# Block-sparse attention stage: softmax denominators exchanged by a VectorE stream shuffle instead of a TensorE product, and four kinds of filler work gathered into later groups

## What is computed

```python
def make_block_sparse_mask(seq_len):
    bi = jnp.arange(seq_len) // BLOCK_SIZE            # blocks of 128
    is_global = bi % GLOBAL_EVERY == 0                # block 0
    allowed = (bi[:, None] == bi[None, :]) | is_global[:, None] | is_global[None, :]
...
scores = jnp.einsum('bhqd,bhkd->bhqk', q * scale, k) + mask
attn = jax.nn.softmax(scores, axis=-1)
out = jnp.einsum('bhqk,bhkd->bhqd', attn, v)
out = out.transpose(0, 2, 1, 3).reshape(B, L, D)
return out @ w_out.T + b_out
```

## Time and profile before

| | |
|---|---|
| median of 3 runs | 3188.89 us (3188.46 to 3190.44) |
| the profiled execution | 3189.74 us, span 3187.9 us |
| TensorE busy in the span | 3000.4 us (94%) |
| VectorE, ScalarE, GpSimd busy | 2341.2, 1703.3, 1696.9 us |
| mean granted TensorE clock | 0.978 of 2.4 GHz |

### The profile page before, as it was taken

The page is one execution under the profiler, slowest core; times in us unless marked ns, Lnnn a source line. Parts: engine busy times, 40 slices in busy tenths (PEclk is TensorE's granted clock), DMA queues, the critical chain, the costliest instruction groups (busy, mean ns, idle before and its releaser), DMA issues. The chain is left out here.

```text
span 3187.9 us, 46188 instructions
## 1 busy us (share of the span) xinstructions
PE 3000.4 (94%) x14226; PEld 1726.6 (54%) x14226; DVE 2341.2 (73%) x4175; ACT 1703.3 (53%) x3501; POOL 1696.9 (53%) x1102
## 2 busy tenths in 40 slices
PE   6999999999999988899999799999999999999997
PEld 3454545454545444455555466666666666666665
DVE  8999999999999988577775655556665555565553
ACT  4767686858586753344444344444444444444442
POOL 2666666666666655233332455555555555565552
PEclk9999999999999999899999799999999999999998
DMA  4767676767667666311010000000001200000000
GB/s 149 256 213 259 215 252 216 243 220 247 231 236 241 214 231 198 97 41 39 26 33 28 20 21 7 13 20 20 20 20 40 73 14 26 20 26 26 26 13 21
DMA packets 131300, 343.37 MB, mean 108 GB/s; under 512 B 14898, under 2 KB 57990, under 8 KB 131222
## 3 DMA queue, kind: packets, MB, share of 16 engines
q1 hardware_dynamic: 128918, 334.02, 30.9%
q10 hardware_dynamic: 2304, 8.39, 0.7%
HBM read 320.87 MB, written 21.50 MB: 107 GB/s over the span
## 5 line engine op out<-in xcount | busy, mean ns | idle before, releaser
L559 POOL TENSOR_TENSOR hb<-bcB,du 128x1024 f32<-128x1024 f32 x256 | 602.5, 2354 | 389.1 <-DVE hb L699 349.9
L688 DVE TENSOR_TENSOR_SCAN ps_dA<-ps_dA,hb 128x1024 f32<-128x1024 f32 x256 | 585.7, 2288 | 43.1 <-ACT ps_dA L914 43.1
L1226 PE MATMUL ps_y<-hb,ident 128*128 128x512 f32 x1024 | 490.4, 608 | 29.6 <-DVE hb L699 29.6
L2375 POOL TENSOR_TENSOR c_pr<-c_pr,c_inv 128x512 f32<-128x512 f32 (+1 forms) x256 | 237.3, 935 | 321.4 <-DVE c_inv L2496 321.4
L914 ACT ACTIVATE ps_dA<-delta,a_neg 128x511 f32<-128x511 f32 x512 | 330.0, 676 | 1.1
L1226 PEld LDWEIGHTS ps_y<-hb,ident 128*128 128x128 f32 x1024 | 189.5, 192 | 251.7 <-issue 186.8
L699 DVE TENSOR_TENSOR hb<-ps_dA,bcC 128x1024 f32<-128x1024 f32 x256 | 311.9, 1218 | 5.9
L2634 ACT ACTIVATE c_pr<-c_ps_s,c_negmax 128x256 f32<-128x256 f32 (+1 forms) x512 | 223.9, 452 | 147.1 <-DVE c_negmax L2489 123.7
L1785 ACT ACTIVATE b_pt<-b_ps_t 128x512 f32<-128x512 f32 x320 | 173.9, 595 | 214.6 <-PE b_ps_t L1905 214.1
L2489 DVE CUSTOM_DVE_ANT_0 c_ps_s<-c_ps_s,c_mask 128x256 f32<-128x256 f32 (+1 forms) x512 | 188.5, 418 | 120.0 <-issue 120.0
L1622 DVE TENSOR_REDUCE b_negmax<-b_ps_s 128x4 f32<-128x1024 f32 (+1 forms) x160 | 194.8, 1222 | 96.6 <-PE b_ps_s L1889 96.5
(11 more groups left out here) (314 smaller groups left out, 5904.2 us busy)
## 6 DMA issues: line engine op xcount, KB each, us to landing
bcB<-bc_scratch SPq DMA_DIRECT2D x256, 512.0 KB, 4.5
bcC<-bc_scratch SPq DMA_DIRECT2D x256, 512.0 KB, 4.6
c_x<-stream_scratch SPq DMA_DIRECT2D x16, 512.0 KB, 4.9
c_xr<-stream_scratch SPq DMA_DIRECT2D x16, 512.0 KB, 3.6
rows<-in_x_dram SPq DMA_DIRECT2D x8, 512.0 KB, 5.4
sum<-in_x_dram SPq DMA_DIRECT2D x8, 512.0 KB, 7.6
x_scratch<-sum SPq DMA_DIRECT2D x8, 512.0 KB, 6.7
b_xb<-x_scratch SPq DMA_DIRECT2D x8, 512.0 KB, 4.6
```

The costliest lines, as they stand in the source:

```text
L559: pool.tensor_tensor(hb[:, s % RING, :, :], bcB[:, s % ROWS, :, :], bc(du[:, c % 2, :].unsqueeze(1), [P, NG, T]), ALU.mult)\
L688: dve.tensor_tensor_scan(flat(h_all), flat(h_all), flat(tile), 0.0, ALU.mult, ALU.add)\
L1226: last = pe.matmul(ps_y[:, :], W["ident"][:, :], hb[:, r % RING, i, :], start=False, stop=(g == GROUPS - 1 and i == NG - 1))
L2375: pool.tensor_tensor(rows, rows, bc(inv[:, u, :].unsqueeze(2), [P, 2, w]), ALU.mult)\
```

## The change

TensorE's permutation (`swap_inverse`, the `b_swap` constant and its masks) is gone. `den` is now written first; VectorE waits for it, writes `num`, and moves `den` by 16 partitions within each 32 with a `stream_shuffle` to `inv`, where the reciprocals are taken in place. The multiplication `divide` moves to GpSimd, behind a `mask`. The product of quarter 0 with v stands in group 4, in front of quarter 1's. The transposes of the next item move to groups 3 and 4, both q/k projections of a half to group 5, all of the projection to v to group 4, its copy to group 4 and the statistics to group 5. In `last`, VectorE shuffles before it inverts and GpSimd multiplies.

```diff
-            return () if m or k > 2 else ((0,), (1, 2), (3,))[k]
-            return (0,) if k == (1 if m else 3) else (1,) if k == (3 if m else 5) else ()
+                    if more and m == 0 and k in (3, 4):
+                        uses += [("x", 2 * (k - 3)), ("x", 2 * (k - 3) + 1)]
+                    if more and k == 5:
+                        uses += [("qk", m, 0), ("qk", m, 1)]
...
+        SWAPPED = [(i + HD) % 32 for i in range(32)]
...
+            def divide(b, m):
+                pool.wait_ge(inv_ready.s, inv_ready.at(b, m + 1))
+                pool.wait_ge(out_done.s, out_done.at(b, 0))
+                pool.tensor_tensor(oT[:, m, :], num[:, :], inv[:, :], ALU.mult).then_inc(oT_ready.s, 1)
...
-                dve.scalar_tensor_tensor(num[:, :], ps_o[:, :], row_mask[:, 1:2], o_num[:, :], ALU.mult, ALU.add)
                 dve.scalar_tensor_tensor(den[:, :], ps_o[:, :], row_mask[:, 0:1], o_den[:, :], ALU.mult, ALU.add)\
                     .then_inc(out_parts.s, 1)
+                dve.wait_ge(out_parts.s, out_parts.at(b, 2 * m + 1))
+                dve.scalar_tensor_tensor(num[:, :], ps_o[:, :], row_mask[:, 1:2], o_num[:, :], ALU.mult, ALU.add)\
+                    .then_inc(out_parts.s, 1)
+                dve.stream_shuffle(inv[:, :], den[:, :], SWAPPED).then_inc(den_swapped.s, 1)
...
-                last = dve.reciprocal(inv[:, cols], den[:, cols])
+                last = dve.reciprocal(inv[:, cols], inv[:, cols])
...
-            def divide(b, m):
-                dve.wait_ge(inv_swapped.s, inv_swapped.at(b, m + 1))
-                dve.wait_ge(out_done.s, out_done.at(b, 0))
-                dve.tensor_tensor(oT[:, m, :], num[:, :], ps_s[:, 0, :], ALU.mult).then_inc(oT_ready.s, 1)
...
-                    if more and k == 5:
+                    if more and k == 4:
                         take_v(n)
-                    if more2 and k == 6:
+                    if more2 and k == 5:
                         statistics(n + 1)
...
-            def swap_inverse(b, m):
-                pe.wait_ge(inv_ready.s, inv_ready.at(b, m + 1))
-                pe.matmul(ps_s[:, 0, :], swap[:, :, :, :].rearrange("p g f d -> p (g f d)"), inv[:, :], start=True, stop=True)\
-                    .then_inc(inv_swapped.s, 1)
...
-                    if k in (2, 4, 6, 8):
+                    if k == 4:
+                        weigh(b, 0, 0, uses, b)
+                    if k in (4, 6, 8):
                         weigh(b, 0, (k - 2) // 2, uses, b)
```

More of the change, by code:

```diff
@@ L1482, in _ @@
             pool.memset(sixteenths[:, :], 0.0).then_inc(s_const, 1)
-            pool.memset(swap[:, :, :, :], 0.0).then_inc(s_const, 1)
-            pool.wait_ge(s_const, 2)
+            pool.wait_ge(s_const, 1)
             pool.affine_select(out=sixteenths[:, :], in_=sixteenths[:, :], compare_op=ALU.not_equal, fill=1.0,
                                base=0, pattern=[[-HD, 8]], channel_multiplier=1).then_inc(s_const, 1)
[L1487 to L1490, removed]
             pool.memset(negmax[:, :, :, :], 0.0).then_inc(s_const, 1)
@@ L1557, in body @@
                     mask(n, 0, 0, USES, b)
+                if prev:
+                    divide(b - 1, 1)
                 part_out(b, 0)
@@ L1569, in body, with last @@
                     mask(n, 1, 1, USES, b)
-            batches(pool, first, body, lambda b: None)
+            def last(b):
+                for t in range(TT):
+                    cols = slice(t * P, (t + 1) * P)
+                    pool.wait_ge(inv_ready.s, inv_ready.at(b, 1) + t + 2)
+                    pool.tensor_tensor(oT[:, 1, cols], num[:, cols], inv[:, cols], ALU.mult).then_inc(oT_ready.s, 1)
+            batches(pool, first, body, last)
         @block.vector
@@ L1728, in last @@
                     .then_inc(out_parts.s, 1)
[L1729 to L1746, removed]
+                dve.wait_ge(out_parts.s, out_parts.at(b, 2 * DC - 1))
+                dve.stream_shuffle(inv[:, :], den[:, :], SWAPPED).then_inc(den_swapped.s, 1)
+                dve.wait_ge(den_swapped.s, den_swapped.at(b, DC))
+                for t in range(TT):
+                    dve.reciprocal(inv[:, cols(t)], inv[:, cols(t)]).then_inc(inv_ready.s, 1)
+                    if t == 0:
+                        dve.scalar_tensor_tensor(num[:, :], ps_o[:, :], row_mask[:, 1:2], o_num[:, :], ALU.mult, ALU.add)\
+                            .then_inc(inv_ready.s, 1)
                 dve.wait_ge(xb_ready.s, xb_ready.at(b, 1))
                 dve.wait_ge(stored.s, stored.at(b, 0))
-                divide_part(2)
-                divide_part(3)
                 for half in range(2):
@@ L1822, in body @@
                             exponents(b, m, k, z, uses["p", m, k, z])
-                        if more:
-                            for h in turned_at(m, k):
+                        if more and m == 0 and k in (3, 4):
+                            for h in (2 * (k - 3), 2 * (k - 3) + 1):
                                 take_x(b + 1, h, b, uses["x", h])
-                            for keys in projected_at(m, k):
+                        if more and k == 5:
+                            for keys in range(2):
                                 take_qk(b + 1, m, keys, b, uses["qk", m, keys])
@@ L1860, in project_qk, with project_v @@
                 last.then_inc(filled.s, 1)
-            def project_v(n, ts):
-                for t in ts:
+            def project_v(n):
+                for t in range(TT):
                     for k in range(DC):
@@ L2060, in last @@
                 for t in range(TT):
-                    pe.wait_ge(inv_ready.s, inv_ready.at(b, 1) + t + 1 + (t > 0))
-                    pe.matmul(bank(t % 2)[:, t * P:(t + 1) * P], swap[:, :, :, :].rearrange("p g f d -> p (g f d)"),
-                              inv[:, t * P:(t + 1) * P], start=True, stop=True).then_inc(inv_swapped.s, 1)
-                    if t:
-                        pe.wait_ge(oT_ready.s, oT_ready.at(b, 1) + t)
-                        last = out_part(t - 1, 1)
-                        if t == 2:
-                            last.then_inc(out_done.s, 1)
-                pe.wait_ge(oT_ready.s, oT_ready.at(b, 1) + TT)
-                out_part(TT - 1, 1).then_inc(out_done.s, 1)
+                    pe.wait_ge(oT_ready.s, oT_ready.at(b, 1) + t + 1)
+                    last = out_part(t, 1)
+                    if t % 2:
+                        last.then_inc(out_done.s, 1)
             batches(pe, first, body, last)
```

55 lines of the change are left out of this document (19 added, 36 removed).

## The result

The changed kernel takes 3218.81 us (median of 4 runs, 3218.77 to 3220.01) against 3189.64 us before (3188.46 to 3190.44): ratio 1.0091, 95% interval 1.0078 to 1.0103, so 29.2 us slower, and outside the predicted range. The profiled execution has a span of 3217.0 us (before 3187.9) and a mean granted TensorE clock of 0.971 (before 0.978).

A forecast was written before the change was run, and what follows sets the result against it. A bare group is bound by VectorE, and only filler makes TensorE the bound. Terms 11.1 - 3.3 + 1.0 - 3.35 - 0.8 = +4.7 us on 3189.74 gave about 3194 us (median), range 3179 to 3208.

The forecast's parts named there:

- rival 3: Thin groups in each half bring TensorE's clock down; one in three halves losing 4 us makes +17, 3211 us; chance 0.05.
- 1.85 - 0.55: Block-sparse stage: each half 0 of items 1 to 6 +1.85 us, each half 1 of items 0 to 5 -0.55 us.
- Groups 3 and 4: Both wait for VectorE's maxima: group 3 starts at 7.5 (half 0) or 5.79 (half 1), group 4 at 7.8 (half 1).
- Groups 7 to 8 stay 2.5 us apart: Group 8 still starts 2.4 to 2.5 us after group 7, waiting for a maximum, so removing the swap gives nothing in half 0.
- The wait for v is gone: Group 6 of half 1: the copy of v fits under group 5, so TensorE's wait of 1.41 us disappears.
- Group 8's scores shorten from 1.30 to 1.08: Half 1, group 8: scores took 1.30 us because ScalarE was behind and should take 1.08, part of the -0.55.
- The shuffle, 0.68: VectorE's shuffle of the denominators, in front of the maximum of index 3, takes 0.6 to 0.7 us.
- GpSimd's multiplication, 1.04: The multiplication moved to GpSimd takes about 1.04 us, hidden by slack in both halves and costed at nothing.
- The end of the stage, -0.8: Stage's end: VectorE no longer waits 0.89 us for TensorE; with an added shuffle and GpSimd's quarter multiplication, -0.8 us.
- 1 (smaller waits): Waits of groups 1 to 3 are smaller than counted and the change is faster, 3179 us; chance 0.20.
- 2 (a dear shuffle): A shuffle of 1.06 us adds 0.4 us in each of 13 halves: 3199 us, or 3206 with a stall; chance 0.13.
- 4 did not come about: The change does nothing beyond order; waits and savings cancel, leaving 3189 us within 2; chance 0.07.

The follow-up runs named there:

- e4: The changed kernel without its shuffle in the halves (a wait and a tiny memset instead, so denominators stand at the wrong partitions): 3194.15 us.
- f5: The changed kernel with the shuffle one place later, behind the maximum of index 3 instead of in front of it: 3193.49 us.
- e2: The kernel before with only the new order of filler; TensorE's swap and VectorE's multiplication stay: 3190.01 us.
- f1: The changed kernel with the key scores of group 2 computed twice into the same place: 3199.07 us.
- e1: The changed kernel with all filler put back in the old order; shuffle and GpSimd's multiplication stay: 3191.26 us.
- f2: e1 plus a product of constants that nobody reads, in group 7 where the swap stood: 3188.57 us.
- f3: The kernel before with all of the projection to v and its copy in group 4, statistics ahead of that copy, swap kept: 3169.89 us.
- g1: f3 plus seven products of 256 columns that nobody reads, in groups 1 to 7 of item 7's last half: 3172.71 us.

## Why the prediction was wrong

**The failed step is rival 3, the clock.** The sum held no term for it. I saw 2 us of wait in 6, and argued that the engine works between the waits and that dense stretches follow; so I gave it a chance of 0.05, and falls in one half out of three. The runs show a fall in every half, 13 of them, which cost 18.2 of the 29.2 us. The price that I had set on this rival, +17 for four us in a third of the halves, is near that only by luck: it is 1.4 us in all of them.

It hangs on a few tenths of a us of wait. Waits for maxima ahead of groups 3 and 4, and the falls in 6 halves 0 and 7 halves 1:

| kernel | half 0: group 3 | half 1: groups 3, 4 | falls in half 0, in half 1 | item, us |
|---|---|---|---|---|
| the change | 1.50 | 0.68, 0.58 | 6, 7 | 61.45 |
| `e4`, no shuffle | 1.11 | 0.29, 0.59 | 1 (twice as long), 0 | 57.79 |
| `f5`, shuffle later | 0.88 | none, 1.37 | 1, 1 | 58.11 |
| `e2`, order alone | 0.75 | none, 0.59 | 0, 0 | 57.09 |
| `f1`, keys twice in group 2 | none | none, 0.59 | 0, 0 | 58.59 |

(An item's time is one without a fall, but for the change, which has none such. Group 2 of a half 0 waits 0.24 us in all five.) In half 0 the falls follow the wait. In half 1 they do not: `f5` waits there for as long as the change, and TensorE is busy for less of the 14.6 us behind the transposes of the maxima (13.19 against 13.33), yet the clock falls in one half 1 of seven instead of in all. A half 1 of the change, then of `f5`, both up to the place of the fall:

```profile
1512.40:1527.00 14.60, 13.33 (x124) 8.87 (x125) 11.29 (x14) 6.23 (x12) 3.92 (x4) 1.00 0.23 72
...
1441.53:1456.13 14.60, 13.19 (x121) 8.74 (x120) 11.27 (x14) 6.51 (x12) 4.01 (x4) 1.00 0.24 72
```

The Trainium skill (TensorE: Matmul & The Clock Gate, Part 1) says that idleness brings the throttle back. The trace agrees: the falls come behind a wait of 1.50 us in half 0, and behind waits of 0.68 and 0.58 us two us apart in half 1. I had the starts to 0.1 us and the rule, and did not put the two together.

**The steps of the sum held, some of them by luck.** An item now takes 61.45 us with two falls, so 61.45 - 2.8 = 58.65 without them, 1.30 more than before, as 1.85 - 0.55 says. (With 1.6 for the fall in half 1 it would be 1.1.) By halves, from one transpose of the maxima to the next, half 0 went from 25.23 to 28.39, which is +1.8 beside a fall (predicted +1.85), and half 1 from 32.12 to 33.07, which is -0.45 (predicted -0.55). In detail:

- *Groups 3 and 4:* group 3 of both halves and group 4 of half 1 start within 0.1 us of what I reckoned; group 4 of half 0 starts at T = 10.0 instead of 9.65, ahead of the fall. The sign that I gave, waits of 1 to 2 us each, came true for group 3 of half 0 alone (1.50).
- *Groups 7 to 8 stay 2.5 us apart, and the swap gives nothing back in half 0:* right, 2.55 us (1570.01 to 1572.56). That the swap was free is now shown by `e1` and `f2`.
- *The wait for v is gone in half 1, group 6:* right; group 7 to group 8 is 2.56 us there (1541.63 to 1544.19).
- *Group 8's scores shorten from 1.30 to 1.08:* wrong; they still take 1.27 to 1.29 us. Group 8 itself comes sooner than I reckoned, at T = 22.7 instead of 23.0 in half 0 and t = 23.6 instead of 23.75 in half 1, when 1.4 us are taken off for the fall. The misses nearly cancel.
- *The shuffle, 0.68:* it is 0.72. *GpSimd's multiplication, 1.04:* it is 1.27, still hidden in the halves; I had taken a row whose second operand is one repeated column.
- *The end of the stage, -0.8:* right. From the last product with v to the next stage it was 13.17 us and is 12.32. But here GpSimd's `b_oT` does release TensorE, which I had named as a sign of being wrong. Most of this wait is VectorE's work ahead of it:

```profile
1787.27 3.79 PE L2026 MATMUL b_ps_s<-gate_up,b_oT 128*128 128x256 f32 x8 [3.73 <-POOL b_oT L1572]
```

The landmarks add up the rest. By the transposes of the maxima in item 0, half 0 (1328.55 before, 1330.86 now), 2.3 us are lost where I had 0. Of these, 1.1 stand there before the stage's first product (1272.33 against 1271.27), in code that did not change. The other 1.2 go with the clock: it is low for some 17 us here in both kernels, before from about 1297.0 to 1314.5 and now from 1301.5 to 1319.0, where less of the time is wait. From the output projection of item 5 to that of item 6 I had 1.0 - 0.85 and a fall would make it 1.55; it is 2.33. From there to the next stage I had -3.3; it is -2.4 (44.16 to 41.79), and the clock is at 0.50 for much of it in both. And 2.3 us are lost behind the stage (1422.2 against 1419.9), in code that did not change. Together: 4.7 of the forecast, 18.2 for the thirteen falls, 1.1 ahead of the stage, 1.2 at item 0, 1.7 in items 6 and 7, 2.3 behind the stage: 29.2.

The 2.3 us behind the stage are not the change's own. In seven of the 14 profiled executions this stretch takes 1421.6 to 1422.2 us, and `f2`, which is as fast as the kernel before, is among them; in the other seven it takes 1418.5 to 1420.4. What goes with it is a low clock some 30 us into the next stage: in the first seven it comes in two pieces (1827.5 to 1838.0 and 1844.5 to 1851.5 in the change), in the others in one (1798.5 to 1819.5 before).

Of the other rivals, 1 (smaller waits) was wrong, since the maxima came as reckoned; 2 (a dear shuffle) was wrong in its price, as 0.04 us more a half is nothing, though the shuffle's place in the queue matters through the clock (`f5`); 4 did not come about.

The large expected gain, 17.8 us of swap and 1.41 us of wait per item, went like this: the swap's time lay in a wait for VectorE and comes back as plain wait (`e1`), and the wait for v was a real gain, spent on waits for maxima 3 and 4 and then more than spent on the clock. `f3` takes the gain without the price.

**Open:** the exact condition for a fall, since neither the longest wait nor TensorE's busy time orders the halves 1 of the change and of `f5`; why one kernel's runs differ in their falls; and what splits the low clock behind the stage.

## What to carry to other kernels

Work that stands in a hole of TensorE's was free here, and removing it can cost: the trace shows it as busy time, and only the distance between starts shows that the hole stays. When filler is gathered, ask what the engine does in the places it leaves: waits of 0.6 to 1.5 us behind thin work can halve the clock for 3.4 us, as they did here, so price one fall (1.4 us here) times the number of places, not as a remote case. If a wait is for VectorE, first look at what stands in its queue ahead of the awaited instruction and needn't: one shuffle moved by one place was worth 25 us, and statistics moved by two groups, with the projection to v gathered, 19.

## What the runs showed of the hardware that was not expected

- Added work made the kernel faster: key scores computed twice in one group of ten saved 19.7 us (`f1` against the change), by the clock.
- A fall is short and sharp: 1.00 to 0.50 and back within some 3.4 us, though TensorE is busy all through the windows of 2 us from 1558 to 1562 in which it is low.
- The response is steep: 0.39 us less wait ahead of group 3 in both halves (`e4`) turned 13 falls into one of double length, in the profiled execution.
- The same wait does not always bring a fall: three of the waits of 2.36 us in `e1` did, and one of the waits of 1.37 us in `f5`.
- Seven idle products of 256 columns held the clock at 1.00 through the last half of item 7 (`g1`), where waits of 0.39 to 0.67 us came ahead of a fall in `f3`.
- A stream shuffle brings a second instruction, `LOAD_MASK_SELECT`, of 0.014 us; no gap on VectorE goes with it.
